# ScalarE takes the squares of adj's tiles after VectorE has turned them, and VectorE no longer waits for it

## What is computed

```python
# layer 0 (N = 5120, D = 64)
e   = concat(par_u0 * par_u1 * (diag_u * x_u @ W_u) + x_u,
             par_i0 * par_i1 * (diag_i * x_i @ W_i) + x_i)
h   = adj @ (adj.T @ e)
out = layer_norm(h) * gamma + beta + x
x   = layernorm(x + out)
# layer 1: two rounds of attention and pruning of adj's edges
edge_scores = softmax(cos(x) * adj, axis=1)
edge_mask   = (edge_scores >= theta) & ...        # theta is 0.000244 or a little more
...
x   = layernorm(x + relu(message over the edges that survive))
```

## Time and profile before

| what | value |
|---|---|
| runs | 421.73, 418.92, 419.19 us; median 419.19 |
| profiled execution | 419.28 us, of which the span is 417.5 us |
| granted TensorE clock over the span | 0.981 |
| busy in the span | PE 390.6, PEld 231.0, DVE 329.2, ACT 230.6, POOL 39.4 us |
| loads of adj | 200 of 512 KB, 107.60 MB read from HBM |

### The profile page before, as it was taken

The page is one execution under the profiler, slowest core; times in us unless marked ns, Lnnn a source line. Parts: engine busy times, 40 slices in busy tenths (PEclk is TensorE's granted clock), DMA queues, the critical chain, the costliest instruction groups (busy, mean ns, idle before and its releaser), DMA issues.

```text
span 417.5 us, 13482 instructions
## 1 busy us (share of the span) xinstructions
PE 390.6 (94%) x5882; PEld 231.0 (55%) x5882; DVE 329.2 (79%) x405; ACT 230.6 (55%) x439; POOL 39.4 (9%) x56
## 2 busy tenths in 40 slices
PE   7989999999999999999999999999999999989900
PEld 6966655644655584465556446555644655555900
DVE  1989999977978796797879679787967978934864
ACT  2759597694199069419906941990694197010310
POOL 5000000000000000000000000000000000492573
PEclk9999999999999999999999999999999999999975
DMA  7999999999977794988779499777959973000012
GB/s 224 349 348 362 386 387 385 386 383 360 325 287 269 259 388 160 341 282 327 264 264 389 161 339 322 287 263 250 382 182 340 320 288 128 3 2 3 2 50 82
DMA packets 61985, 109.85 MB, mean 263 GB/s; under 512 B 3936, under 2 KB 14304, under 8 KB 61920
## 3 DMA queue, kind: packets, MB, share of 16 engines
q1 hardware_dynamic: 61248, 108.80, 73.3%
q10 hardware_dynamic: 672, 0.12, 0.2%
HBM read 107.60 MB, written 1.31 MB: 261 GB/s over the span
## 4 chain that ended last, share of the span: by engine, by line
PE 82%; SPq 8%; POOL 3%; DVE 3%; DMA 2%; issue 1%; ACT 1%; DVEq 0%
PE pair L1340 40%; PE pair L1307 38%; SPq L959 7%; PE pair L1323 2%; DMA pooled<-in_adj 2%; POOL pooled L1030 2%; POOL pooled L1025 2%; PE pair L1353 1%; DVE pooled L1221 1%; SPq L946 1%; DVE pooled L1242 0%; DVE pooled L1231 0%; DVE pooled L1181 0%; DVE pooled L1183 0%; DVE pooled L1213 0%
## 5 line engine op out<-in xcount | busy, mean ns | idle before, releaser
L1162 DVE STREAM_TRANSPOSE pooled<-pooled 128x1024 f32<-128x1024 f32 x200 | 229.8, 1210 | 4.8 <-PE pair L1307 4.1
L1062 ACT ACTIVATE scratch<-pooled 128x1024 bf16<-128x1024 f32 x200 | 208.4, 1049 | 2.8 <-DMA pooled<-in_adj 2.6
L1307 PE MATMUL pair<-pooled,rows_in 128*64 128x256 f32 (+1 forms) x1760 | 181.6, 362 | 1.9 <-DMA pooled<-in_adj 1.9
L1340 PE MATMUL pair<-pooled,col_sum 32*64 32x512 f32 (+1 forms) x3840 | 180.0, 519 | 2.1 <-ACT col_sum L1072 1.2
L1307 PEld LDWEIGHTS pair<-pooled,rows_in 128*64 128x64 f32 x1760 | 119.8, 137 | 69.2 <-issue 19.1
L1340 PEld LDWEIGHTS pair<-pooled,col_sum 32*64 32x64 f32 x3840 | 84.2, 131 | 85.9 <-issue 79.0
L1183 DVE TENSOR_TENSOR pooled<-pooled,pair 128x512 f32<-128x512 f32 (+1 forms) x120 | 63.4, 588 | 61.3 <-PE pair L1340 61.3
L1072 ACT COPY col_sum<-pair 128x512 f32<-128x512 f32 (+1 forms) x22 | 11.0, 550 | 132.1 <-PE pair L1323 132.1
L1062 ACT ACTIVATION_READ_ACCUMULATOR scratch<-pooled 128x1 f32 x200 | 38.5, 192 | 0.0
L1011 POOL TENSOR_SCALAR pooled<-pooled 128x40 f32<-128x40 f32 x1 | 0.3, 316 | 352.0 <-DVE pooled L1203 352.0
L1093 ACT ACTIVATE pooled<-pair 128x512 f32<-128x512 f32 x5 | 3.0, 595 | 18.8 <-PE pair L1353 18.8
(11 more groups left out here) (52 smaller groups left out, 73.0 us busy)
## 6 DMA issues: line engine op xcount, KB each, us to landing
pooled<-in_adj SPq DMA_DIRECT2D x200, 512.0 KB, 9.3
pooled<-in_x SPq DMA_DIRECT2D x5, 256.0 KB, 5.2
out<-pooled SPq DMA_DIRECT2D x5, 256.0 KB, 2.0
pooled<-in_x SPq DMA_DIRECT2D x1, 768.0 KB, 5.1
pooled<-in_x SPq DMA_DIRECT2D x1, 512.0 KB, 3.7
pooled<-in_w_ui ACTq DMA_DIRECT2D x2, 32.0 KB, 5.5
beta_sb<-in_beta ACTq DMA_DIRECT2D x1, 32.0 KB, 5.9
pooled<-in_diag ACTq DMA_DIRECT2D x1, 20.0 KB, 5.0
```

The source lines that it names most:

```text
L1062: nc.scalar.activation(scratch[v % 2][:, :], slots[slot_of(v)], ACT.Square, accum_out=square_sum[:, v:v + 1]).then_inc(unit_scanned, 1)
L1162: nc.vector.transpose(tiles, tiles).then_inc(unit_turned, 1)
L1307: mm = pe.matmul(block_bank[c % 2][half(h), 0:w // 2], rows_in[:, t, :], slots[slot_of(v)][:, at:at + w // 2], start=(t == 0), stop=(t == ...
L1340: mm = pe.matmul(round_banks(g)[a][half(b % 2), 0:w].rearrange("p (t r) -> p t r", r=32), col_sum[g // RPB % 2][quadrant(a), b, :], to[qua ...
```

## The change

```diff
-    BOUND = 0.2
-    assert math.exp(BOUND + 0.01) < THETA[0] * (N - math.sqrt(N * NB) * BOUND) and THETA[0] <= min(THETA)
+    BOUND = 0.165
+    assert math.exp(BOUND + 0.01) < THETA[0] * (N - math.sqrt(N * NB * 32) * BOUND) and THETA[0] <= min(THETA)
     LIMIT = BOUND * BOUND
...
                 if before:
                     sp.wait_ge(round_done, round_of_unit(before[-1]) + 1)
+                    sp.wait_ge(unit_scanned, before[-1] + 1)
...
             def scan(v):
-                wait_loaded(act, v)
+                act.wait_ge(unit_turned, v + 1)
                 if v >= 2:
                     act.wait_ge(unit_scanned, v - 1)
...
-            for k in range(LGROUPS - 1):
+            for k in range(LGROUPS):
                 copy_pairs(k)
-            scan(0)
-            copy_pairs(LGROUPS - 1)
-            for v in range(1, UNITS):
+            for v in range(UNITS):
                 c, i = place_of_unit(v)
                 scan(v)
-                if v == UPB[0] - 1:
+                if v == 5:
                     act.wait_ge(gamma_turned, 1)
                     act.copy(center[:, D:2 * D], bank[0][:, 0:D]).then_inc(center_kept, 1)
                     keep_cols(0)
-                if c >= 2 and i == 1:
-                    keep_cols(c - 1)
-            keep_cols(NB - 1)
+                if c and i == UPB[c] - 1:
+                    keep_cols(c)
...
                 dve.wait_ge(unit_used, v + 1)
-                dve.wait_ge(unit_scanned, v + 1)
```

## The result

Over 19 runs each, the changed kernel takes 421.53 us (420.98 to 424.55), the kernel before 419.16 us (418.82 to 421.98). The ratio is 1.0055, 95% interval 1.0039 to 1.0072: slower by half a per cent, clear of noise, and 0.5 us above the range that was forecast. The profiled execution has a span of 419.7 us, 2.2 us more than before.

A forecast was written before the change was run, and what follows sets the result against it. PE, busy throughout the middle (321.81 us), was taken as the bound. Profiled 419.28 us, plus 0.2 for the last block, minus 0, gave 419.48; that execution stood 0.09 above the median, so 419.4 us, range 418.1 to 421.0.

The forecast's parts named there:

- The wait that goes: Start-up, DVE no longer waits for ACT at 31.51 us: turns 0.66 us earlier, gain used up by 43.03; term 0.
- The wait that comes: ACT's scans now wait for DVE's turns: ACT, the faster, stays at most one unit behind once caught up before block 2.
- the copies at the block's end: Copies move behind each block's last scan; PE's work multiplied ahead covers them; term 0 for blocks 0 to 9.
- The rival of a ScalarE that falls behind by whole units: At block ends PE waits for late copies, 1.04 us per unit; over 1% slower from four units; chance 0.03.
- The last block: End of the last block, without cover: copies start 0.2 us later and delay PE; term 0.2, between 0 and 1.2 us.
- SyncE's second wait: SyncE's 160 loads: an always satisfied wait, 0.24 us per round's eight loads, hidden; term 0, at most 4.8 us.
- paragraph on the rest: Remaining edits, such as copying `center` behind the sixth scan: same addresses, instruction count and scans; ACT's and DVE's work unchanged.
- The rule of the Trainium skill on extra semaphore instructions: Waiting for several engines may add semaphore instructions: charges SP's 160 loads, relieves DVE's 200 turns; neither on the path.
- The rival on the slower side: ACT falls behind and PE waits for block-end copies: over 1% slower; chance 0.03 by four units, slower overall 0.04.
- something of under 1% not seen: Anywhere in the kernel: an unforeseen effect of under 1%; chance 0.02.

The follow-up runs named there:

- E1: The kernel before with only SyncE's second wait added, ahead of each of its 160 loads into a used slot: 421.31 us, ratio 1.0047.
- E3: The kernel before with 160 instructions of already satisfied waits on SyncE, in one place behind the last load of adj: 421.42 us, ratio 1.0053.

## Why the prediction was wrong

Its sum stopped where its views stopped. Step by step:

- **The wait that goes.** Right to a few hundredths: the fifth turn starts at 30.88 with no wait (30.85 said), the addition of round 0 up by 0.29 us (0.3 said), the next one at 43.03, PE's stall 0.84 us.
- **The wait that comes, and the copies at the block's end.** Right. At block 2 the copies were forecast to end at 79.93; ACT's row is below, it ends at 79.97, and PE starts at 83.22 as before. At block 5 they end at 187.12 (187.2 said). The rival of a ScalarE that falls behind by whole units didn't happen anywhere.

```profile
78.92 1.05 ACT L1074 COPY col_sum<-pair 128x512 f32<-128x512 f32 x2
```

- **The last block.** Right in kind, 0.10 us where 0.2 was taken: the copies start at 368.71, 0.13 us later and not 0.2, and this trace has DVE's last turns 0.09 us earlier.
- **SyncE's second wait: the step that failed.** The prediction said "It still is an instruction", priced it as time in SyncE's queue (0.03 us each, 0 to 4.8 us in all), and set the term to 0 because the loads have cover. The queue time is in fact covered (E1's middle stretch). What it left out is that 160 instructions also move everything behind them in SyncE's list, the last branch and its target among them. That term measured 2.1 and 2.2 us (E1, E3) and is 0 for 10, 20, 128 or 256 instructions. It lies inside the 0 to 4.8 us written down for the edit, but those were the bounds of another mechanism, and the range didn't take them in. Its paragraph on the rest even says "same number of instructions", against its own "It still is an instruction".
- **What made it possible.** The forecast compared all terms with the chain of waits, whose last piece ends at 413.14, while the span ends at 417.5. The 4.3 us between were never asked about. SyncE stood in them as the last engine, with no cover for anything.
- **The rule weighed for it.** The rule of the Trainium skill on extra semaphore instructions ("Perfetto Trace Analysis", section "Identifying Dependency Chains") was cited and said to be on no path. The trace agrees with the rule to the instruction: 160 more on SyncE, 200 fewer on VectorE, 13482 less 40 are 13442. The conclusion drawn from it was wrong.
- **The chances.** The rival on the slower side, with 0.04, had another mechanism. The loss of 0.55% is inside the 1% that the text called no change, and 0.02 was kept for something of under 1% not seen; this is where it belongs. The text took 1% as what a measurement can tell apart; 19 runs tell half a per cent.

## What to carry to other kernels

Count the instructions that an edit adds to or takes from each engine's list, waits included, and look at what branches behind them: a few waits can move a jump's target out of what the engine holds (32 did here, 20 didn't), for 2.1 us. Read the trace from the last computation to the end of the span; an engine that takes a branch there, behind the last store, has no cover. Where a branch can be taken earlier, beside a transfer's landing, take it there; where it can't, a difference of some 2 us between two kernels with the same timeline is to be checked by padding before it is put down to the edit.

## What the runs showed beside that

- The step of a taken branch differs by engine in every kernel: before, GpSimd 0.17 us, SyncE 0.48, ScalarE 2.65, VectorE 3.48, TensorE 3.94. Only SyncE's step moved between two values in these runs. VectorE's stayed long when its branch moved by 200 (3.48 us before, 3.52 in the changed kernel); no run was made to move the other engines' branches.
